# The feed-forward layer of a fused Perceiver kernel: both products as three fp32r passes, accumulated tile by tile in four banks

## The chip, the cores and the metric

The kernel runs on one core of one Trainium2 chip. The metric is the device time of one launch in microseconds (us). The engines are PE (TensorE, matrix products), ACT (ScalarE), DVE (VectorE), POOL (GpSimd) and SP (SyncE, which issues the DMAs). Each runs its own instruction list in order; they wait for each other through semaphores.

## What is computed

Six layers act on 1024 tokens of width 512 (16 batches of 64), one after the other: a cosine cross-attention, a self-attention, a mixture of experts, a cross-attention, a decayed attention and a feed-forward layer. Only the last one matters here. Its part of the reference, in short:

```python
def pwlin_gelu_basic(x, mantissa_bits_in, mantissa_bits_out):
    xq = float2fix(x, mantissa_bits_in)          # rounded to multiples of 2^-8
    y = jnp.interp(xq, _PWL_X, _PWL_Y)           # exact GELU at 33 knots on [-4, 4]
    y = jnp.where(xq > 4.0, xq, jnp.where(xq < -4.0, 0.0, y))
    return float2fix(y, mantissa_bits_out)

h = layernorm(x) @ w1 + b1        # w1 is 512 x 2048
h = pwlin_gelu_basic(h, 8, 8)
y = float2fix(h @ w2 + b2, 8)     # w2 is 2048 x 512
out = x + y
```

All of it is fp32. The tokens lie in SBUF as 8 tiles `x[:, t, :]` of 128 tokens by 512.

## The kernel before

`feed_forward_layer` splits the tokens into two groups of four tiles (`NGR` = 2, `TG` = 4) and the inner width into 16 tiles of 128 (`FT`). One step n, of `N` = 32, is one inner tile of one group: 128 inner rows by 512 tokens. A step is this pipeline:

- PE, `hidden(n)`: four fp32 products `w16` by `xT[g]` into PSUM bank n mod 3.
- ACT, `stage_a(n)`: `h` (L2004) out of PSUM, then `r` (L2009), both 128x512.
- DVE, `round_(n)`: `c` (L2047) and `up` (L2051), clamped forms of `r`.
- ACT, `stage_b(n)`: `km` (L2019, the knot), then GELU at both neighbouring knots, `g0` (L2022) and `g1` (L2024).
- POOL, `slope(n)`: `dg` = g1 - g0 (L1943).
- DVE, `interpolate(n)`: three operations on `y` (L2060, L2063, L2065; the second one waits for `dg`) and then `hs` (L2067), the finished inner tile.
- PE, `output(t, f0, f1)`: token tile t by the inner tiles f0 to f1-1, fp32, into bank 3 + t mod 3.

The inner tiles of both groups are kept in SBUF (`hs`, 2 x 16 tiles). The order on PE is written out by hand: the transposes of the first group's normalized tokens, the 16 `hidden` steps of group 0 (with the transposes of group 1 at four places among them), then 16 times a `hidden` step of group 1 and four `output` products of group 0, and last the 64 `output` products of group 1. DVE and ACT interleave two steps: DVE runs `round_(n + 1)` ahead of `interpolate(n)`, ACT `stage_a(n + 1)` ahead of `stage_b(n)`. `Norm` computes the layer norm: DVE statistics (L134 to L137), a power on POOL (L142), `xn` on DVE (L148), four transposes on PE (L155) into bank 7, and a copy `xT` on ACT (L1998). DVE normalizes the second group's tiles after steps 1, 3, 5 and 7. `finish(t)` takes an output tile out of PSUM with three DVE operations (L2075, L2077, L2078), and SP stores it with two DMAs.

`split_product` (L103, used by other layers before and by this one after) does an fp32 product as three passes of the faster type fp32r: with each operand as a first part (rounded to fp32r) and a rest, it adds first x first, first x rest and rest x first. ACT makes the first part by a copy, DVE the rest by a subtraction.

At the start of the layer's block SP issues the loads of `b1`, `w26` (4 MB) and `b2`, in this order; DVE waits for both biases before it does anything else in the layer. `w16` is loaded during the layer before.

## Time and profile before

| | us |
|---|---|
| median of 3 runs (2247.7 to 2256.31) | 2249.49 |
| the profiled execution's own time | 2252.86 |
| its span, from first to last instruction | 2251.0 |
| PE busy over the span | 2014.5 |
| DVE busy | 1085.9 |
| ACT busy | 914.2 |
| POOL busy | 100.5 |

The feed-forward layer is the last eighth: its loads are issued at 1983.7 us of the span, and the program ends at 2251.0. A row of the timeline gives start, duration, engine, line and operation, with what it writes and reads; in square brackets stands how long the engine had been idle before it and who ended that. Operations of one engine overlap by their tails, so the distance of two starts can be under the first one's duration. A PE row merges several matmuls. An fp32 product is recorded as two matmuls, an fp32r product as one.

### The profile page before, as it was taken

How to read it: one execution, taken by the hardware profiler on the slowest of the kernel's cores; microseconds unless marked ns; L12 is line 12 of the kernel's file. 1: busy time of each engine (PE TensorE's matmuls, PEld its weight loads, DVE VectorE, ACT ScalarE, POOL GpSimd, SP SyncE). 2: the span in 40 equal slices, each digit the busy share in tenths (PEclk: the TensorE clock that was granted, in tenths of full speed). 3: DMA queues.
4: the chain of work that ended last, by engine and by line, in shares of the span. 5: the costliest groups of instructions: out<-in, count | busy, mean ns of one | idle time of the engine just before them, and what ended most of it. 6: DMA issues, size and time to landing. Idle time of an engine off the chain costs nothing. (4 is left out here: it accounts for less than half of the span.)

```text
span 2251.0 us, 29109 instructions
## 1 busy us (share of the span) xinstructions
PE 2014.5 (89%) x9936; PEld 1418.6 (63%) x9936; DVE 1085.9 (48%) x2233; ACT 914.2 (41%) x1684; POOL 100.5 (4%) x113
## 2 busy tenths in 40 slices
PE   7978963999999959999999999999968898858998
PEld 5647763555555547777778787878746676623443
DVE  5665651001010127363544445363538899929852
ACT  5743320111111125353544444454526667726650
POOL 0000002000000001000000000000000000002220
PEclk9989875999999989999999999999988888779999
DMA  7410006777777622110101100000212000020000
GB/s 266 135 46 1 0 17 245 289 313 312 293 297 313 261 71 76 38 47 14 47 14 47 43 31 33 28 33 28 75 63 103 1 1 1 1 80 1 5 10 24
DMA packets 33156, 208.19 MB, mean 92 GB/s; under 512 B 4546, under 2 KB 4674, under 8 KB 25540
## 3 DMA queue, kind: packets, MB, share of 16 engines
q1 hardware_dynamic: 30532, 199.02, 23.5%
q0 software_dynamic: 2560, 8.39, 1.1%
q8 instruction: 31, 0.51, 0.1%
q14 instruction: 33, 0.27, 0.0%
HBM read 186.95 MB, written 20.45 MB: 92 GB/s over the span
## 5 line engine op out<-in xcount | busy, mean ns | idle before, releaser
L109 PE MATMUL PS<-cT,qs 128*128 128x512 f32 x1152 | 293.9, 401 | 9.0 <-ACT pb L1259 7.0
L109 PE MATMUL PS<-pT,cN 128*128 128x512 f32 x1152 | 271.8, 394 | 1.7 <-DVE pT L1354 1.7
L109 PEld LDWEIGHTS PS<-cT,qs 128*128 128x128 f32 x1152 | 208.6, 188 | 59.3 <-issue 15.0
L917 PE MATMUL PS<-W,xgT 128*128 128x384 f32 x736 | 243.7, 490 | 1.4 <-ACT xgT L940 1.4
L109 PEld LDWEIGHTS PS<-pT,cN 128*128 128x128 f32 x1152 | 215.1, 189 | 45.8 <-DVE pT L1354 1.9
L917 PEld LDWEIGHTS PS<-W,xgT 128*128 128x128 f32 x736 | 141.1, 192 | 104.4 <-issue 12.1
L109 PE MATMUL PS<-ws,xT 128*128 128x512 f32 x672 | 180.4, 427 | 6.4 <-DVE ws L563 4.9
L109 PEld LDWEIGHTS PS<-ws,xT 128*128 128x128 f32 x672 | 137.6, 207 | 45.8 <-issue 11.5
L1349 DVE TENSOR_REDUCE nmax<-PS 128x1 f32<-128x512 f32 x128 | 87.7, 685 | 156.0 <-PE PS L109 155.6
L968 DVE TENSOR_TENSOR hid<-gated,PS 128x384 f32<-128x384 f32 x46 | 23.4, 551 | 278.4 <-PE PS L893 235.6
L1254 ACT ACTIVATE qp<-PS 128x512 f32<-128x512 f32 x96 | 57.4, 598 | 191.4 <-PE PS L109 191.4
L901 PE MATMUL PS<-W,hT 128*128 128x512 f32 x276 | 124.5, 601 | 10.3 <-ACT hT L934 10.3
L1962 PE MATMUL PS<-xT,W 128*128 128x512 f32 x256 | 118.4, 613 | 1.3 <-ACT xT L1998 0.8
L1354 DVE TENSOR_TENSOR pT<-PS,pT 128x512 fp32r<-128x512 f32 x128 | 86.9, 684 | 54.6 <-ACT pT L1276 54.6
L947 ACT ACTIVATE gated<-PS 128x384 f32<-128x384 f32 x46 | 20.0, 488 | 228.2 <-PE PS L917 228.2
L1972 PE MATMUL PS<-W,hs 128*128 128x512 f32 x256 | 112.5, 592 | 0.0
L1566 PEld LDWEIGHTS PS<-cn,W 128*128 128x128 f32 x512 | 77.8, 225 | 39.0 <-DVE W L1878 31.6
L155 PE MATMUL PS<-cn,xn 128*128 128x128 f32 x160 | 28.8, 310 | 81.9 <-DVE xn L148 72.9
L1276 ACT ACTIVATE pT<-PS 128x512 fp32r<-128x512 f32 x128 | 75.6, 597 | 64.3 <-PE PS L1154 64.1
L1259 ACT ACTIVATE pb<-PS,nmax 128x512 f32<-128x512 f32 x128 | 87.5, 684 | 34.5 <-DVE nmax L1349 34.4
L1566 PE MATMUL PS<-cn,W 128*128 128x16 f32 x512 | 76.6, 284 | 24.2 <-DVE W L1878 24.0
L901 PEld LDWEIGHTS PS<-W,hT 128*128 128x128 f32 x276 | 50.6, 190 | 70.7 <-issue 56.9
(231 smaller groups left out, 3096.5 us busy)
## 6 DMA issues: line engine op xcount, KB each, us to landing
W<-in_fc SPq DMA_DIRECT2D x23, 3072.0 KB, 12.4
W<-in_proj SPq DMA_DIRECT2D x23, 1536.0 KB, 6.5
cT<-in_ctxT SPq DMA_DIRECT2D x16, 768.0 KB, 5.2
ct_in<-in_ctxT SPq DMA_DIRECT2D x16, 768.0 KB, 4.2
cn_in<-in_ctxN SPq DMA_DIRECT2D x16, 768.0 KB, 5.1
W<-in_w SPq DMA_DIRECT2D x2, 4096.0 KB, 12.9
routed_x<-zero SPq DMA_DIRECT2D x23, 256.0 KB, 5.4
xg<-routed_x SPq DMA_DIRECT2D x23, 256.0 KB, 5.6
```

The source lines that it names most:

```text
L109: mm = nc.tensor.matmul(out, lhs(m, s), rhs(n, s), start=(opens and (s, m, n) == terms[0]), stop=((s, m, n) == terms[-1]))
L155: last = self.nc.tensor.transpose(self.bank[:, k * P:(k + 1) * P], self.xn[:, k * P:(k + 1) * P], self.ident)
L901: mm = nc.tensor.matmul(ps[7], hT[:, f, :], pj[u][:, f, :], start=(f == 0), stop=(f == FK - 1))
L917: mm = nc.tensor.matmul(ps[c][:, 0:HFE], xgT[:, k, :], fc[u][:, k, c * HFE:(c + 1) * HFE], start=(k == 0), stop=(k == DK - 1))
L1254: nc.scalar.activation(out, src, ACT.Copy, scale=scale).then_inc(w_sb, count)
L1259: nc.scalar.activation(pb[:, g % 2, :], ps[g % 2], ACT.Exp, bias=nmax[:, g % 4:g % 4 + 1], accum_out=rsum[:, g % 4:g % 4 + 1]).then_inc(e_ ...
L1276: nc.scalar.activation(turned(pT[0], g), ps[2 + g % 2].rearrange("p (j n) -> p j n", j=JK), ACT.Copy).then_inc(pt_hi, 1)
L1349: nc.vector.tensor_reduce(nmax[:, g % 4:g % 4 + 1], ps[g % 2], AX.X, ALU.max, negate=True).then_inc(m_dve, 1)
L1354: return nc.vector.tensor_tensor(out, whole, first.bitcast(F32), ALU.subtract)
L1566: mm = nc.tensor.matmul(ps[6 + c % 2][:, col:col + B], rb[:, t % RB, k * P:(k + 1) * P], sel, start=True, stop=True)
L1962: mm = nc.tensor.matmul(ps[n % HB], w16[:, k, f * P:(f + 1) * P], xT[g][:, k, :], start=(k == 0), stop=(k == DK - 1))
L1972: mm = nc.tensor.matmul(ps[HB + t % ZB], hs[:, t // TG, f, (t % TG) * P:(t % TG + 1) * P], w26[:, f, :], start=(f == 0), stop=(f == FT - 1))
```

## The change

The whole change is inside `feed_forward_layer`. Both products go through three fp32r passes. The inner tile is no longer kept: each step's finished `hs` is split into `hp` (first part by ACT, L2037, rest by DVE, L2112), and PE multiplies it four steps later (`LAG`) by the matching rows of `w26` into four banks at once, one for each token tile of the group, which accumulate over the 16 steps of a group. The weights are split for each step as well, into rings of three: `ws` for the first product (ACT L2004, DVE L2107, two steps ahead) and `vs` for the second (ACT L2044, DVE L2117). The normalized tokens are split as they leave PSUM (`rest_x`). Since a weight is split again in each group, every step has three more copies on ACT and three more subtractions on DVE. The group's four banks are read by `sum_out` (L2126) in one go after step 18, and finished one each after steps 19 to 22; those of the second group at the end. `b2` is loaded ahead of `w26`, and DVE waits for the biases after the norms of the first four tiles.

How the steady step's rows move on two engines. First DVE, one step of the second group, as it stood before (`c`, `up`: clamps of the next step; `y`, `hs`: this step's interpolation):

```order
L2047 TENSOR_SCALAR c<-r 128x512
L2051 TENSOR_SCALAR up<-r 128x512
L2060 SCALAR_TENSOR_TENSOR y<-km,c 128x512
L2063 SCALAR_TENSOR_TENSOR y<-y,dg 128x512
L2065 SCALAR_TENSOR_TENSOR y<-g,y 128x512
L2067 SCALAR_TENSOR_TENSOR hs<-y,up 128x512
```

and as it stands now, where `ws`, `hp` and `vs` are the rests of the first weight, of the inner tile and of the second weight:

```order
L2117 TENSOR_TENSOR vs<-W,vs 128x512
L2075 TENSOR_SCALAR c<-r 128x512
L2079 TENSOR_SCALAR up<-r 128x512
L2107 TENSOR_TENSOR ws<-W,ws 128x512
L2112 TENSOR_TENSOR hp<-hs,hp 128x512
L2089 SCALAR_TENSOR_TENSOR y<-km,c 128x512
L2092 SCALAR_TENSOR_TENSOR y<-y,dg 128x512
L2094 SCALAR_TENSOR_TENSOR y<-g,y 128x512
L2096 SCALAR_TENSOR_TENSOR hs<-y,up 128x512
```

Between one step's `hs` and the next one's first `y` DVE had two operations; now it has five. On ACT, one step before:

```order
L2004 ACTIVATE h<-PS,b1q 128x512
L2009 ACTIVATE r<-h,cn 128x512
L2019 ACTIVATE km<-c,cn 128x512
L2022 ACTIVATE g<-km,cn 128x512
L2024 ACTIVATE g<-km,cn 128x512
```

and now, where `ws`, `hp` and `vs` are the first parts:

```order
L2004 ACTIVATE ws<-W 128x512
L2010 ACTIVATE h<-PS,b1q 128x512
L2015 ACTIVATE r<-h,cn 128x512
L2037 ACTIVATE hp<-hs 128x512
L2025 ACTIVATE km<-c,cn 128x512
L2028 ACTIVATE g<-km,cn 128x512
L2030 ACTIVATE g<-km,cn 128x512
L2044 ACTIVATE vs<-W 128x512
```

The copy `hp<-hs`, which waits for `hs` of the step before, stands ahead of `km` and the two GELUs. Before, nothing on ACT waited for `hs` of the step before.

The diff, without the declarations of semaphores and the removed bodies of `output` and `finish`, which the listing of the kernel before shows:

```diff
--- before.py
+++ after.py
...
-        hs = sbuf("hs6", [P, NGR, FT, 512])
-        xT = [sbuf(f"xT6{g}", [P, DK, TG * P]) for g in range(NGR)]
+        WR, LAG = 3, 4
+        hs = sbuf("hs6", [P, 2, 512])
+        hp = [sbuf(f"hp6{part}", [P, WR, 512], F32R) for part in range(2)]
+        vs = [sbuf(f"vs6{part}", [P, WR, D], F32R) for part in range(2)]
+        xT = [[sbuf(f"xT6{g}{part}", [P, DK, TG * P], F32R) for part in range(2)] for g in range(NGR)]
+        ws = [sbuf(f"ws6{part}", [P, WR, DK, P], F32R) for part in range(2)]
+        z = sbuf("z6", [P, TG, D])
...
-        z = x[:, NT, :]
...
-        TURN_LAG, OUT_LAG = 6, 4
+        TURN_LAG, OUT_LAG = 4, 3
...
                 sp.dma_start(b1[:, :], a["b16"]).then_inc(s_b, 16)
+                sp.dma_start(b2[:, :], a["b26"]).then_inc(s_b, 16)
                 sp.dma_start(w26, a["w26"]).then_inc(s_w26, 16)
-                sp.dma_start(b2[:, :], a["b26"]).then_inc(s_b, 16)
...
                     g, f = divmod(n, FT)
                     if f == 0:
                         pe.wait_ge(ln.xT_ready, BASE + TG * (g + 1))
+                    pe.wait_ge(w_lo, BASE + n + 1)
                     if n >= HB:
                         pe.wait_ge(h_sb, BASE + n - HB + 1)
-                    for k in range(DK):
-                        mm = nc.tensor.matmul(ps[n % HB], w16[:, k, f * P:(f + 1) * P], xT[g][:, k, :],
-                                              start=(k == 0), stop=(k == DK - 1))
-                    mm.then_inc(h_mm, 1)
-                def output(t, f0, f1):
...
+                    split_product(nc, ps[n % HB], lambda part, k: ws[part][:, n % WR, k, :],
+                                  lambda part, k: xT[g][part][:, k, :], DK).then_inc(h_mm, 1)
+                def output(n):
+                    g, f = divmod(n, FT)
+                    pe.wait_ge(hp_lo, BASE + n + 1)
+                    pe.wait_ge(v_lo, BASE + n + 1)
+                    for t in range(TG):
+                        if g and f == 0:
+                            pe.wait_ge(z_used, BASE + t + 1)
+                        for m, r in ((0, 0), (0, 1), (1, 0)):
+                            mm = nc.tensor.matmul(ps[HB + t], hp[m][:, n % WR, t * P:(t + 1) * P], vs[r][:, n % WR, :],
+                                                  start=(f == 0 and m == r), stop=(f == FT - 1 and m == 1))
+                    mm.then_inc(o_mm, 1)
...
-                for n in range(FT):
+                for n in range(N):
                     hidden(n)
                     if n - TURN_LAG in NORM_AT:
                         ln.tensor(pe, TG + NORM_AT.index(n - TURN_LAG))
...
+                    if n >= LAG:
+                        output(n - LAG)
+                for n in range(N - LAG, N):
+                    output(n)
...
                     act.wait_ge(ln.turned, BASE + t + 1)
-                    part = xT[t // TG][:, :, t % TG * P:(t % TG + 1) * P]
-                    nc.scalar.activation(part, ps[7].rearrange("p (k t) -> p k t", k=DK),
-                                         ACT.Copy).then_inc(ln.xT_ready, 1)
+                    part = xT[t // TG][0][:, :, t % TG * P:(t % TG + 1) * P]
+                    nc.scalar.activation(part, ps[7].rearrange("p (k t) -> p k t", k=DK), ACT.Copy).then_inc(x_hi, 1)
+                def first_w(n):
+                    if n >= WR:
+                        act.wait_ge(h_mm, BASE + n - WR + 1)
+                    nc.scalar.activation(ws[0][:, n % WR, :, :], w16[:, :, n % FT * P:(n % FT + 1) * P],
+                                         ACT.Copy).then_inc(w_hi, 1)
...
+                def first_h(n):
+                    act.wait_ge(hs_sb, BASE + n + 1)
+                    if n >= WR:
+                        act.wait_ge(o_mm, BASE + n - WR + 1)
+                    nc.scalar.activation(hp[0][:, n % WR, :], hs[:, n % 2, :], ACT.Copy).then_inc(hp_hi, 1)
+                def first_v(n):
+                    if n == 0:
+                        act.wait_ge(s_w26, BASE + 16)
+                    if n >= WR:
+                        act.wait_ge(o_mm, BASE + n - WR + 1)
+                    nc.scalar.activation(vs[0][:, n % WR, :], w26[:, n % FT, :], ACT.Copy).then_inc(v_hi, 1)
+                act.wait_ge(e.s_w6, BASE + 16)
+                first_w(0)
+                first_w(1)
                 for t in range(TG):
                     norm_out(t)
                 act.wait_ge(b_q, BASE + 2)
                 stage_a(0)
                 for n in range(N):
+                    if n + 2 < N:
+                        first_w(n + 2)
                     if n + 1 < N:
                         stage_a(n + 1)
+                    if n:
+                        first_h(n - 1)
                     stage_b(n)
+                    first_v(n)
                     if n - OUT_LAG in NORM_AT:
                         norm_out(TG + NORM_AT.index(n - OUT_LAG))
+                first_h(N - 1)
...
                     ve.wait_ge(km_sb, BASE + n + 1)
                     if n >= 2:
                         ve.wait_ge(hs_sb, BASE + n - 1)
+                        ve.wait_ge(hp_lo, BASE + n - 1)
...
-                    nc.vector.scalar_tensor_tensor(hs[:, g, f, :], y[:, u, :], ROUND, up[:, u, :], ALU.add,
+                    nc.vector.scalar_tensor_tensor(hs[:, u, :], y[:, u, :], ROUND, up[:, u, :], ALU.add,
                                                    ALU.add).then_inc(hs_sb, 1)
+                def rest_x(t):
+                    ve.wait_ge(x_hi, BASE + t + 1)
+                    hi, lo = (part[:, :, t % TG * P:(t % TG + 1) * P] for part in xT[t // TG])
+                    nc.vector.tensor_tensor(lo, ps[7].rearrange("p (k t) -> p k t", k=DK), hi.bitcast(F32),
+                                            ALU.subtract).then_inc(ln.xT_ready, 1)
+                def rest_w(n):
+                    ve.wait_ge(w_hi, BASE + n + 1)
+                    nc.vector.tensor_tensor(ws[1][:, n % WR, :, :], w16[:, :, n % FT * P:(n % FT + 1) * P],
+                                            ws[0][:, n % WR, :, :].bitcast(F32), ALU.subtract).then_inc(w_lo, 1)
+                def rest_h(n):
+                    ve.wait_ge(hp_hi, BASE + n + 1)
+                    nc.vector.tensor_tensor(hp[1][:, n % WR, :], hs[:, n % 2, :], hp[0][:, n % WR, :].bitcast(F32),
+                                            ALU.subtract).then_inc(hp_lo, 1)
+                def rest_v(n):
+                    ve.wait_ge(v_hi, BASE + n + 1)
+                    nc.vector.tensor_tensor(vs[1][:, n % WR, :], w26[:, n % FT, :], vs[0][:, n % WR, :].bitcast(F32),
+                                            ALU.subtract).then_inc(v_lo, 1)
+                def sum_out(t):
+                    g = t // TG
+                    ve.wait_ge(o_mm, BASE + FT * (g + 1))
+                    if g:
+                        ve.wait_ge(x_done, BASE + t - TG + 1)
+                    nc.vector.tensor_tensor(z[:, t % TG, :], ps[HB + t % TG], b2[:, :], ALU.add).then_inc(z_used, 1)
                 def finish(t):
+                    zt = z[:, t % TG, :]
+                    ve.wait_ge(z_used, BASE + t + 1)
+                    ch.link(nc.vector.tensor_scalar(zt, zt, ROUND, ROUND, ALU.add, ALU.subtract))
+                    nc.vector.scalar_tensor_tensor(x[:, t, :], zt, 1.0 / QUANT, x[:, t, :], ALU.mult,
+                                                   ALU.add).then_inc(x_done, 1)
+                for t in range(TG):
+                    ln.vector_stats(ch, t)
                     if t:
...
+                        rest_x(t - 1)
+                    ln.vector_norm(ve, t)
                 ve.wait_ge(s_b, BASE + 32)
                 nc.vector.tensor_scalar(b1q[:, :], b1[:, :], QUANT, None, ALU.mult).then_inc(b_q, 1)
                 nc.vector.tensor_scalar(b2[:, :], b2[:, :], QUANT, None, ALU.mult).then_inc(b_q, 1)
-                for t in range(TG):
-                    ln.vector_stats(ch, t)
-                    ln.vector_norm(ve, t)
+                rest_w(0)
+                rest_w(1)
+                rest_x(TG - 1)
                 round_(0)
                 for n in range(N):
                     if n + 1 < N:
                         round_(n + 1)
+                    if n + 2 < N:
+                        rest_w(n + 2)
+                    if n:
+                        rest_h(n - 1)
                     interpolate(n)
+                    rest_v(n)
                     if n in NORM_AT:
                         ln.vector_stats(ch, TG + NORM_AT.index(n))
                         ln.vector_norm(ve, TG + NORM_AT.index(n))
...
+                    if n - OUT_LAG in NORM_AT:
+                        rest_x(TG + NORM_AT.index(n - OUT_LAG))
+                    if n == FT + 2:
+                        for t in range(TG):
+                            sum_out(t)
+                    elif FT + 3 <= n < FT + 3 + TG:
+                        finish(n - FT - 3)
+                rest_h(N - 1)
+                for t in range(TG, NT):
+                    sum_out(t)
                     finish(t)
```

## Rows read from the trace of the kernel before

**Rows 1.** Windows: stretch, us, busy PE, PEld, DVE, ACT, POOL, then PEclk, DMA.

```profile
2026.64:2197.73 171.09, 162.15 (x383) 71.41 (x382) 134.14 (x210) 100.84 (x152) 42.05 (x35) 0.99 0.02 5
2197.73:2251.00 53.27, 47.54 (x111) 20.75 (x109) 8.96 (x16) 0.00 (x0) 0.00 (x0) 0.98 0.08 25
```

**Rows 2.** Chain that ended last: start, us, what.

```profile
2101.07 3.43 PE PS L1962 x8
...
2189.91 55.38 PE PS L1972 x129
```

**Rows 3.** Timeline from the layer's loads to the first finished step.

```profile
1983.71 0.33 SPq L1926 DMA_DIRECT2D b<-in_b  x1
...
1997.01 0.18 DVE L2082 TENSOR_SCALAR b1q<-b 128x16 f32<-128x16 f32 x1 [14.51 <-DMA b<-in_b]
...
1997.43 0.69 DVE L134 BATCH_NORM_STATS2 st<-x 128x6 f32<-128x512 f32 x1
...
1999.30 0.55 DVE L148 TENSOR_SCALAR xn<-x,mv,rs 128x512 f32<-128x512 f32 x1 [0.66 <-POOL rs L142]
...
2001.05 0.60 ACT L1998 ACTIVATE xT<-PS 128x512 f32<-128x512 f32 x1 [23.03 <-PE PS L155]
...
2008.77 21.54 PE L1962 MATMUL PS<-xT,W 128*128 128x512 f32 x44 [0.78 <-ACT xT L1998]
...
2025.95 0.69 DVE L2067 SCALAR_TENSOR_TENSOR hs<-y,up 128x512 f32<-128x512 f32 x1
```

**Rows 4.** Timeline of PE in the cross-attention: a dense fp32r stream.

```profile
1617.59 8.46 PE L109 MATMUL PS<-pT,cN 128*128 128x512 f32 x36
1625.89 2.21 PE L109 MATMUL PS<-cT,qs 128*128 128x512 f32 x9
```

**Rows 5.** Timeline in the cross-attention: splits into first part and rest.

```profile
1071.51 0.63 ACT L1267 ACTIVATE cT<-ct_in 128x512 fp32r<-128x512 f32 x1
1071.80 0.68 DVE L1354 TENSOR_TENSOR cT<-ct_in,cT 128x512 fp32r<-128x512 f32 x1
1072.04 0.68 ACT L1259 ACTIVATE pb<-PS,nmax 128x512 f32<-128x512 f32 x1
```

**Rows 6.** Timeline of one feed-forward step: DVE, ACT, POOL.

```profile
2107.33 0.41 DVE L2047 TENSOR_SCALAR c<-r 128x512 f32<-128x512 f32 x1
...
2107.78 0.72 ACT L2019 ACTIVATE km<-c,cn 128x512 f32<-128x512 f32 x1 [0.98 <-DVE c L2047]
2108.00 0.68 DVE L2060 SCALAR_TENSOR_TENSOR y<-km,c 128x512 f32<-128x512 f32 x1
...
2109.17 0.71 ACT L2024 ACTIVATE g<-km,cn 128x512 f32<-128x512 f32 x1
...
2109.95 1.31 POOL L1943 TENSOR_TENSOR dg<-g 128x512 f32<-128x512 f32 x1 [3.09 <-ACT g L2024]
2110.17 1.64 DVE L2067 SCALAR_TENSOR_TENSOR hs<-y,up 128x512 f32<-128x512 f32 x1
```

**Rows 7.** Timeline a step later: POOL starts while DVE is in an operation.

```profile
2114.57 0.69 DVE L2067 SCALAR_TENSOR_TENSOR hs<-y,up 128x512 f32<-128x512 f32 x1
...
2114.91 1.48 POOL L1943 TENSOR_TENSOR dg<-g 128x512 f32<-128x512 f32 x1 [3.65 <-ACT g L2024]
...
2115.18 1.49 DVE L2047 TENSOR_SCALAR c<-r 128x512 f32<-128x512 f32 x1
```

**Rows 8.** Timeline of PE at an idle time.

```profile
2070.85 0.63 PE L155 MATMUL PS<-cn,xn 128*128 128x128 f32 x4 [3.02 <-ACT xT L1998]
2071.34 12.56 PE L1962 MATMUL PS<-xT,W 128*128 128x512 f32 x24
```

**Rows 9.** Windows of PE just behind it: us, busy, PEclk.

```profile
2072.00:2074.00 2.00, 2.00 (x4) 0.50 0.00 0
```

**Rows 10.** Timeline of DVE: the last output tile.

```profile
2245.37 0.69 DVE L2075 TENSOR_TENSOR x<-PS,b 128x512 f32<-128x512 f32 x1 [11.85 <-PE PS L1972]
...
2246.56 0.69 DVE L2078 SCALAR_TENSOR_TENSOR x<-x 128x512 f32<-128x512 f32 x1
```

More of the change, by code:

```diff
@@ L1912, in feed_forward_layer @@
             sem(n) for n in ("h_mm6", "h_sb6", "r_sb6", "c_sb6", "km_sb6", "g_sb6", "up_sb6", "dg_sb6", "hs_sb6"))
-        z_mm, z_used, x_done, s_out = sem("z_mm6"), sem("z_used6"), sem("x_done6"), sem("s_out6")
+        o_mm, z_used, x_done, s_out = sem("o_mm6"), sem("z_used6"), sem("x_done6"), sem("s_out6")
+        x_hi, w_hi, w_lo = sem("x_hi6"), sem("w_hi6"), sem("w_lo6")
+        hp_hi, hp_lo, v_hi, v_lo = sem("hp_hi6"), sem("hp_lo6"), sem("v_hi6"), sem("v_lo6")
         s_w26 = sem("s_w26")
         N = NGR * FT
-        HB, ZB = 3, 3
+        HB = 3
         NORM_AT = [1 + 2 * t for t in range(TG)]
-        TURN_LAG, OUT_LAG = 6, 4
+        TURN_LAG, OUT_LAG = 4, 3
         e.open_sems()
@@ L1958, in hidden @@
                         pe.wait_ge(ln.xT_ready, BASE + TG * (g + 1))
+                    pe.wait_ge(w_lo, BASE + n + 1)
                     if n >= HB:
                         pe.wait_ge(h_sb, BASE + n - HB + 1)
-                    for k in range(DK):
-                        mm = nc.tensor.matmul(ps[n % HB], w16[:, k, f * P:(f + 1) * P], xT[g][:, k, :],
-                                              start=(k == 0), stop=(k == DK - 1))
-                    mm.then_inc(h_mm, 1)
-                def output(t, f0, f1):
-                    if f0 == 0 and t >= ZB:
-                        pe.wait_ge(z_used, BASE + t - ZB + 1)
-                    for f in range(f0, f1):
-                        pe.wait_ge(hs_sb, BASE + FT * (t // TG) + f + 1)
-                        mm = nc.tensor.matmul(ps[HB + t % ZB], hs[:, t // TG, f, (t % TG) * P:(t % TG + 1) * P],
-                                              w26[:, f, :], start=(f == 0), stop=(f == FT - 1))
-                    if f1 == FT:
-                        mm.then_inc(z_mm, 1)
+                    split_product(nc, ps[n % HB], lambda part, k: ws[part][:, n % WR, k, :],
[11 more added lines that the diff above has]
+                    mm.then_inc(o_mm, 1)
                 for t in range(TG):
                     ln.tensor(pe, t)
-                pe.wait_ge(e.s_w6, BASE + 16)
-                for n in range(FT):
+                for n in range(N):
                     hidden(n)
@@ L1983, in _ @@
                         ln.tensor(pe, TG + NORM_AT.index(n - TURN_LAG))
-                per = FT // TG
-                pe.wait_ge(s_w26, BASE + 16)
-                for f in range(FT):
-                    hidden(FT + f)
-                    output(f // per, f % per * per, (f % per + 1) * per)
-                for t in range(TG, NT):
-                    output(t, 0, FT)
+                    if n >= LAG:
+                        output(n - LAG)
+                for n in range(N - LAG, N):
+                    output(n)
             @block.scalar
@@ L2094, in _ @@
                         ln.vector_norm(ve, TG + NORM_AT.index(n))
-                    per = FT // TG
-                    if n >= FT + 1 and (n - FT) % per == 1 and (n - FT) // per >= 1:
-                        finish((n - FT) // per - 1)
-                for t in range(TG - 1, NT):
+                    if n - OUT_LAG in NORM_AT:
[8 more added lines that the diff above has]
+                    sum_out(t)
                     finish(t)
```

7 lines of the change are left out of this document (removed).

## Prediction

> **What bounds the kernel now.** The edit lies in the last eighth of the span, so I read that layer alone, in three views. The windows cut it in three. From the end of the first finished inner tile (`hs` of step 0, 2026.64) to that of the last (2197.73) both PE and DVE are loaded: PE 162.15 and DVE 134.14 of 171.09 us. After that DVE is nearly empty (8.96) and PE alone works for 53.27 us [rows 1]. The chain that ended last is there PE and nothing else: 129 records of the second product in 55.38 us, and further up alternating blocks of 8 records at 3.43 us. A record is thus 0.429 us, an fp32 product two of them, 0.86 us; a step of the second half, four products in and four out, is 6.86 us of PE [rows 2]. The timeline shows a third stretch ahead of both: DVE stands 14.51 us, to 1997.01, for a bias that is queued behind the 4 MB of `w26`; the first product starts at 2008.77 [rows 3].
>
> **The layer's start.** Without that wait the norms can start right after the loads are issued at 1983.71; I take 1984.0. The first `xn` comes 1.87 later (1997.43 to 1999.30 before), the copy out of PSUM 1.75 after its `xn`, and takes 0.60 [rows 3]. New is the rest on DVE, 0.68 for this shape [rows 5], and the next `xn` stands behind it: a tile now takes 1.75 + 0.60 + 0.03 + 0.61 = 3.0. So four tiles end at 1984.0 + 1.87 + 3 x 3.0 + 1.75 + 0.60 + 0.72 = 1997.9, and PE starts 10.8 earlier. From there to the first `hs` before took 2025.95 + 0.69 - 2008.77 = 17.9 [rows 3]. PE starts at half clock either way; 12 fp32r products (below) take 5.1 there against the 6.2 of the four fp32 ones. With the next weight's rest ahead of the first `y` I get 16.5, so `hs` of step 0 ends at **2014.4**. `w26` is first needed at about 2010; before, a transfer queued behind it had landed by 1997.
>
> **The steady step.** PE: in the cross-attention 36 fp32r matmuls of 128x512 start at 1617.59 and the next group at 1625.89: 8.30 us, 0.231 each [rows 4]. A step has 24, so 5.53 us instead of 6.86. The fp32r passes do save, but only 1.33 per step.
>
> DVE gets three subtractions of 0.68, each 0.61 to the next start (0.61 is the distance from `hs` to `c`) [rows 5, 7]. Its other work: `c` and `up` 0.67 together (2107.33 to 2108.00), the three `y` 2.17 (2108.00 to 2110.17), `hs` 0.61 [rows 6, 7]. Sum: 0.67 + 2.17 + 0.61 = 3.45 old, + 1.83 new = 5.28. That alone would be under PE's 5.53. But a step also has POOL's `dg`, 1.27 when it is not held up (the 1.48 less the 0.21 until the `hs` of 2114.57 has run 0.55), and DVE and POOL do not run side by side here: `hs` that starts 0.22 after `dg` takes 1.64 instead of 0.69 [rows 6], and `dg` that starts inside an `hs` takes 1.48, with the `c` behind it 1.49 instead of 0.41 [rows 7]. Each time the later one ends as if it had begun when the other let go (about 0.55 into a DVE operation). The Trainium skill (SBUF — State Buffer, section "SBUF: two separate sides") has the rule: GpSimd's operation and a VectorE operation with two SBUF inputs take one shared port pair exclusively. By it every new subtraction of the weights and of `hs` is of the kind that cannot overlap `dg`; the trace agrees for the old ones.
>
> Where does `dg` fall now? ACT's new order puts the copy of `hs` of the step before ahead of `km`. Counted from the end of that `hs`: copy at 0.03, 0.53 long to the next start [rows 5], `km`, 1.39 to `g1` (2107.78 to 2109.17), 0.71 for it, 0.07 to POOL [rows 6]: `dg` asks at 2.73. DVE by then: the second weight's rest from -0.08, `c` 0.53, `up`, the first weight's rest 1.20, the rest of `hs` 1.81, `y` 2.42. `dg` gets in when that `y` lets go, 2.97, ends at 4.24, and the second `y` starts about 0.1 later, 4.34; `hs` ends 1.45 + 0.69 later: **6.48 us a step**. Bounds: 6.23 if `dg` could run beside `y` (2.73 + 1.27 + 0.10 + 2.14, ACT's chain alone), 6.9 if handoffs cost what nothing here shows. I take 6.48, since rows 6 and 7 both show the exclusion. So the step's limit moves from PE to a loop DVE - ACT - POOL - DVE, and ACT, nearly idle before, is in it.
>
> A second loop stays just below: first weight's rest ends 1.89, 12 products take 2.94, `h` and `r` some 1.45, and the next copy of `hs` stands behind `r` on ACT: at 6.26, where the first loop has it at 6.48 + 0.03. It has 0.25 to spare.
>
> **What is added on top.** Four norms stand between `hs` and the next `c`: 1.87 + 0.46 [rows 3] and nothing covers them; they also delay the weight's rest by as much, so that `r` is 1 us late a step on: another 0.7. Less small overlaps 2.9 each, 11.6, and 0.6 for the last `rest_x`: 12.2. The four `sum_out` in a row (4 x 0.61) cost 2.3 and the four `finish` 1.0 each: 6.2. The last two steps lack weights to split, -0.5. Steps: 31 x 6.48 = 200.9; together 218.8, against 171.1 before.
>
> **Clock.** PE idles long wherever DVE hands over a weight late: in a step behind a norm the weight's rest ends at 5.3 after `hs` instead of 1.9, while PE has run out of work at about 1.2, so 4 us. That is so ahead of products 2, 3 and 4 (no output products to fill in yet), behind three norms and behind `sum_out`. One idle of 3.02 before was followed by a granted clock of 0.50, the 1.2 GHz level, and 24 records took 12.56 where 24 x 0.429 = 10.3: about 2.1 lost [rows 8, 9]. I take three such drops of some seven chances, 6.3, since they fall on the second loop, which has no room: last `hs` at 2014.4 + 218.8 + 6.3 = **2239.5**. The Trainium skill (TensorE: Matmul & The Clock Gate, section "What's actually happening") says that idleness brings the lower level and activity the higher; by it all seven would drop, which is the second rival below.
>
> **The end.** Where 53.3 us of PE stood alone, only one step is left: copy and rest of `hs` 1.4, 12 products 2.9, then four output tiles on DVE at (2246.56 - 2245.37) + 0.61 = 1.8 each, 7.3, and from the end of DVE's last operation (2247.25) to 2251.0 as before 3.75 [rows 10]: 15.4.
>
> **Sum**, against the profiled execution's own span of 2251.0: start -12.2, steps 218.8 + 6.3 - 171.1 = +54.0, end 15.4 - 53.3 = -37.9: **+3.9**, span 2254.9. The median of the runs shown is 1.5 below that span, so I predict 2253. A difference of 0.5%, 11 us, is about what a measurement of this kernel can tell from none: 2238 to 2261 is "same".
>
> **Rivals.**
> - *Faster* (0.20): `dg` overlaps the subtractions after all, the step is 6.23, and DVE's idle 0.7 a step soaks up part of norms and sums (9 x 0.7): 31 x 6.23 + 18.4 - 6.3 = 205.2 instead of 218.8, and later weights come earlier, so few drops: 2235 span, 2234. For it: no subtraction from fp32 to fp32r ran beside a `dg` before. Against: rows 6 and 7.
> - *Slower by the clock* (0.17): each of the idle times drops the clock, and the 0.95 us of idle in ordinary steps brings some more, 12 in all: +9 x 2.1, 2272. It decides from seven drops on. For it: rows 8 and 9. Against: PE is busy 85% of a step, more than the stretches behind which no drop shows.
> - *Slower by the handoffs* (0.15): a step has six more waits between ACT, DVE and PE; 0.3 us a step of them on either loop is +9.3, 2263. For it: both loops are full. Against: the waits in rows 6 cost 0.03 to 0.10 each and are in the sum.
> - *The forecast* (0.48): own range 2243 to 2264.
>
> **How the numbers follow.** The forecast's case gives 0.02 faster, 0.40 same, 0.06 slower; the faster rival 0.20 faster; the clock 0.14 slower and 0.03 same; the handoffs 0.15 slower. Together 0.22, 0.43, 0.35. The range leaves out about one in ten on either side: 2233 takes in the faster rival, 2275 the clock's.
>
> **What would show it.** First `hs` ending near 2014; `hs` 6.5 apart in steps 10 to 17 and 24 to 29, with the second `y` waiting for POOL about 1.2 and `dg` taking about 1.5 (0.25 of it waiting); PE busy 85% there; norms 9 us a step; 15 us after the last `hs`. It is wrong if `hs` stands 6.25 or 6.8 apart, if PEclk is under 0.9 over the layer, or if the norms still start at 1997.

## The result, and the profile after

The changed kernel takes 2258.18 us (median of 20 runs, 2255.22 to 2262.49), the kernel before 2253.59 in the same series (median of 20). One launch of the kernel before took 7014.76 us and does not enter the ratio. The ratio is 1.0026, with a 95% interval of 1.0019 to 1.0033: slower by a quarter of a per cent, 5.8 us by the means and 4.6 by the medians, which is inside the 0.5% that the prediction called "same". Forecast were 2253 us, and a chance of 0.43 for "same". Of the 5.2 us between that forecast and the measured 2258.18, 4.1 are the base: the forecast started from a median of 2249.49 for the kernel before, which is 2253.59 over 20 runs.

The profiled run took 2256.09 us, its span is 2254.2. The page's line of busy times for it:

```profile
PE 1985.5 (88%) x10192; PEld 1469.4 (65%) x10192; DVE 1137.1 (50%) x2337; ACT 967.3 (43%) x1780; POOL 104.1 (5%) x113
```

PE has 29 us less work than before, DVE 51 and ACT 53 us more. The saving on PE was real and bought nothing.

The layer's length is the measure here: from SP's first load to the end of the span it was 2251.0 - 1983.71 = 267.3 us. Now, from the timeline around the layer's first load:

```profile
1981.40 0.33 SPq L1931 DMA_DIRECT2D b<-in_b  x1
1981.45 0.69 DVE L134 BATCH_NORM_STATS2 st<-x 128x6 f32<-128x512 f32 x1 [1.56 <-PEq L2222]
1983.32 0.55 DVE L148 TENSOR_SCALAR xn<-x,mv,rs 128x512 f32<-128x512 f32 x1 [0.66 <-POOL rs L142]
```

The wait of 14.51 us for the bias [rows 3] is gone: the statistics start 0.05 behind the load's issue. The length is 2254.2 - 1981.40 = 272.8, 5.5 more than before. (That the layer begins 2.3 earlier than in the profile of before is no effect of the edit, nothing ahead of it changed; over all runs here this point lies between 1977.5 and 1985.3.)

One step of the second group, the timeline of DVE, ACT, POOL and PE:

```profile
2106.57 0.69 DVE L2096 SCALAR_TENSOR_TENSOR hs<-y,up 128x512 f32<-128x512 f32 x1
...
2107.30 0.63 ACT L2037 ACTIVATE hp<-hs 128x512 fp32r<-128x512 f32 x1
...
2109.20 3.06 PE L109 MATMUL PS<-xT,ws 128*128 128x512 f32 x12 [0.73 <-DVE ws L2107]
2109.66 0.69 DVE L2089 SCALAR_TENSOR_TENSOR y<-km,c 128x512 f32<-128x512 f32 x1
...
2109.99 1.50 POOL L1948 TENSOR_TENSOR dg<-g 128x512 f32<-128x512 f32 x1 [4.98 <-ACT g L2030]
...
2111.60 0.69 DVE L2092 SCALAR_TENSOR_TENSOR y<-y,dg 128x512 f32<-128x512 f32 x1 [1.26 <-POOL dg L1948]
...
2113.05 0.69 DVE L2096 SCALAR_TENSOR_TENSOR hs<-y,up 128x512 f32<-128x512 f32 x1
```

Two `hs` stand 2113.05 - 2106.57 = 6.48 apart, and so they do (6.47 to 6.49) in steps 12 to 18 and 24 to 29, a step being counted from the `hs` before to its own. In this one `dg` takes 1.50 instead of the 1.27 that it needs alone, and the second `y` stands 1.26 for it. PE, once the bound, waits 0.73 for the weight's rest. The waits over the whole layer (who waited for whom: total, times, longest) tell the same:

```profile
ACT h L2010 <- PE PS L109: 66.0, 32, 6.7
...
PE PS L109 <- DVE ws L2107: 37.3, 26, 4.2
DVE y L2092 <- POOL dg L1948: 34.0, 24, 2.7
```

The first is idle time of ACT, which binds nothing in the steady steps. The second and third are PE and DVE, the two loaded engines, both waiting now.

### The profile page after: what moved, and what is told of

It is laid out like the page before. It is cut to its first block and busy times, and to the rows that moved or that the text cites. A ratio compares the mean times of both kernels' runs of the same rounds, so it can differ in the third digit from the quotient of the medians.

```text
span 2254.2 us, 29909 instructions
## 1 busy us (share of the span) xinstructions
PE 1985.5 (88%) x10192; PEld 1469.4 (65%) x10192; DVE 1137.1 (50%) x2337; ACT 967.3 (43%) x1780; POOL 104.1 (5%) x113
## 5 line engine op out<-in xcount | busy, mean ns | idle before, releaser
L109 PE MATMUL PS<-xT,ws 128*128 128x512 f32 x384 | 108.7, 438 | 39.5 <-DVE ws L2107 37.3
L109 PEld LDWEIGHTS PS<-xT,ws 128*128 128x128 f32 x384 | 78.3, 211 | 69.0 <-DVE ws L2107 49.3
L1979 PE MATMUL PS<-vs,hp 128*128 128x512 f32 x384 | 97.3, 405 | 7.1 <-DVE hp L2112 4.3
```

The source lines that it names most:

```text
L109: mm = nc.tensor.matmul(out, lhs(m, s), rhs(n, s), start=(opens and (s, m, n) == terms[0]), stop=((s, m, n) == terms[-1]))
L1979: mm = nc.tensor.matmul(ps[HB + t], hp[m][:, n % WR, t * P:(t + 1) * P], vs[r][:, n % WR, :], start=(f == 0 and m == r), stop=(f == FT - 1 ...
```

## The experiments

A ratio is always to the kernel before, run on the same chip. "First to last `hs`" is the distance between the first and the last finished inner tile: 171.1 us before [rows 1], 225.6 after.

**1. The new start alone, on the kernel before.**

```diff
-                sp.dma_start(w26, a["w26"]).then_inc(s_w26, 16)
                 sp.dma_start(b2[:, :], a["b26"]).then_inc(s_b, 16)
+                sp.dma_start(w26, a["w26"]).then_inc(s_w26, 16)
...
-                ve.wait_ge(s_b, BASE + 32)
-                nc.vector.tensor_scalar(b1q[:, :], b1[:, :], QUANT, None, ALU.mult).then_inc(b_q, 1)
-                nc.vector.tensor_scalar(b2[:, :], b2[:, :], QUANT, None, ALU.mult).then_inc(b_q, 1)
                 for t in range(TG):
...
                     ln.vector_norm(ve, t)
+                ve.wait_ge(s_b, BASE + 32)
+                nc.vector.tensor_scalar(b1q[:, :], b1[:, :], QUANT, None, ALU.mult).then_inc(b_q, 1)
+                nc.vector.tensor_scalar(b2[:, :], b2[:, :], QUANT, None, ALU.mult).then_inc(b_q, 1)
```

> The kernel before with the start of the new one alone: b2 loaded ahead of w26, and the biases awaited after the first four norms. Theory: the norms start some 13.5 us earlier, the whole layer behind them shifts, 13 us less than before (ratio 0.994). Rival: the earlier start is given back at a later wait (the second weight's load, the DVE-bound first half): no difference.

Measured: 2236.76, ratio 0.9933 (0.9919 to 0.9946). First to last `hs` is 171.1 as before; the gain is all ahead of it. The first `hs` starts 28.6 us after the loads' issue instead of 42.2, 13.7 earlier. The start is worth 15 us by the ratio (12 to 18 by its interval).

**2. New start and new order of PE's work, but both products in fp32 and nothing split** (a ring of 16 `hs`).

```diff
-                for n in range(FT):
+                for n in range(N):
                     hidden(n)
...
+                    if n == LAG:
+                        pe.wait_ge(s_w26, BASE + 16)
+                    if n >= LAG:
+                        output(n - LAG)
+                for n in range(N - LAG, N):
+                    output(n)
```

> The new start and the new order (output product of each step four steps later, four banks, sums after step 18), but both products stay fp32 and nothing is split. Theory: PE is then busy without a break at 6.86 us a step and only one step and four sums are left at the end: 20 us less than before (ratio 0.991), while the fp32r version is 0.26% slower, so the three passes and not the order take the time away. Rival: the order itself is what costs (sums in a row, four banks, waits): no better than before.

Measured: 2232.43, 0.9907 (0.9891 to 0.9922). In the steady steps PE works without a break, eight records (four products) of either kind every 3.43 us, 6.87 a step. From its timeline:

```profile
2150.15 3.60 PE L1963 MATMUL PS<-xT,W 128*128 128x512 f32 x8
2153.58 3.60 PE L1974 MATMUL PS<-W,hs 128*128 128x512 f32 x8
```

So the order costs nothing; it gives another 0.0026. The two intervals just meet, but the layers of the profiled runs say the same: 248.2 us here, 253.7 in number 1. From 0.9907 to 1.0026 the difference is the three passes with their splits and buffers (and the second group's transposes, placed two steps earlier on PE and one on ACT, which was not tried alone): they cost 0.0119, 27 us, though each step of PE needs 1.3 us less.

**3. A second subtraction on POOL behind each `dg`**, of `b2` from itself into a place that nothing reads. It leaves the result as it is.

```diff
+                    if n == 0:
+                        pool.wait_ge(b_q, BASE + 2)
+                    if n:
+                        pool.wait_ge(s_idle, BASE + n)
+                    nc.gpsimd.tensor_tensor(idle, b2[:, :], b2[:, :], ALU.subtract).then_inc(s_idle, 1)
```

> The changed kernel with a second, unused POOL subtraction of the same size behind each dg; nothing waits for it. Theory (DVE and POOL exclude each other): DVE's y or hs of that moment is held up by it, the steady step goes from 6.48 to 7.4 to 7.8 us, 30 to 40 us more. Rival (the step is ACT's and POOL's latency alone): the step stays 6.48, since the added operation lies in POOL's idle time.

Measured in a single run: 2280.37; a step takes 7.22 to 7.25, and the layer is 27.0 us longer than in the changed kernel where I expected 30 to 40. From the timeline of DVE and POOL:

```profile
2119.91 1.52 POOL L1949 TENSOR_TENSOR dg<-g 128x512 f32<-128x512 f32 x1 [4.72 <-ACT g L2036]
...
2121.39 1.04 POOL L1955 TENSOR_TENSOR x<-b 128x512 f32<-128x512 f32 x1
2121.53 1.44 DVE L2098 SCALAR_TENSOR_TENSOR y<-y,dg 128x512 f32<-128x512 f32 x1 [1.27 <-POOL dg L1949]
```

Nobody waits for the added operation, and yet DVE's `y`, starting 0.14 behind it, takes 1.44 instead of 0.69. That is the step's whole increase, 0.75. It came out under the 7.4 to 7.8 that I expected; this subtraction took 1.04, not 1.27, which accounts for 0.23 of it. The exclusion that the prediction took from rows 6 and 7 is there.

**4. `dg` computed by DVE instead of POOL**, whose `slope(n)` is gone.

```diff
-                    ve.wait_ge(dg_sb, BASE + n + 1)
+                    ve.wait_ge(g_sb, BASE + 2 * n + 2)
+                    ch.link(nc.vector.tensor_tensor(dg[:, u, :], g1[:, u, :], g0[:, u, :], ALU.subtract))
+                    ve.sem_inc(dg_sb, 1)
```

> The changed kernel with dg computed by DVE instead of POOL. Theory: dg costs DVE 0.72 instead of 1.27 plus handoffs plus 0.25 of waiting; DVE's own work becomes 6.0 us a step and the second loop (weight rest, 12 products, h, r, copy of hs) binds at 6.2: 8 to 10 us less than the changed kernel, so even with before (ratio 0.998 to 1.000). Rival (DVE's sum of work is already the limit): the step gets longer by 0.6, 20 us more than the changed kernel (ratio 1.011).

Measured: 2241.32, 0.9948 (0.9934 to 0.9961), 17 us under the changed kernel and about twice the 8 to 10 that I expected. One step of DVE, from its timeline:

```profile
2115.88 0.68 DVE L2110 TENSOR_TENSOR vs<-W,vs 128x512 fp32r<-128x512 f32 x1
2116.48 0.42 DVE L2066 TENSOR_SCALAR c<-r 128x512 f32<-128x512 f32 x1
2116.82 0.42 DVE L2070 TENSOR_SCALAR up<-r 128x512 f32<-128x512 f32 x1
2117.15 0.68 DVE L2100 TENSOR_TENSOR ws<-W,ws 128x512 fp32r<-128x512 f32 x1
2117.76 0.68 DVE L2105 TENSOR_TENSOR hp<-hs,hp 128x512 fp32r<-128x512 f32 x1
2118.36 0.68 DVE L2080 SCALAR_TENSOR_TENSOR y<-km,c 128x512 f32<-128x512 f32 x1
2119.07 0.69 DVE L2083 TENSOR_TENSOR dg<-g 128x512 f32<-128x512 f32 x1
2119.91 0.69 DVE L2085 SCALAR_TENSOR_TENSOR y<-y,dg 128x512 f32<-128x512 f32 x1
2120.64 0.69 DVE L2087 SCALAR_TENSOR_TENSOR y<-g,y 128x512 f32<-128x512 f32 x1
2121.37 0.69 DVE L2089 SCALAR_TENSOR_TENSOR hs<-y,up 128x512 f32<-128x512 f32 x1
2121.98 0.68 DVE L2110 TENSOR_TENSOR vs<-W,vs 128x512 fp32r<-128x512 f32 x1
```

No row has a wait in brackets: DVE alone fills 2121.98 - 2115.88 = 6.10. On DVE `dg` costs 0.84 to the next start, on POOL it kept DVE away for 1.26 more than its own work. What I had expected to stop the step at 6.26, the "second loop", does not.

**5. ACT's copy of `hs` behind the GELUs, its rest behind the interpolation**; `dg` stays on POOL.

```diff
+                    stage_b(n)
                     if n:
                         first_h(n - 1)
-                    stage_b(n)
...
+                    interpolate(n)
                     if n:
                         rest_h(n - 1)
-                    interpolate(n)
```

> The changed kernel with ACT's copy of hs moved behind km and the two GELUs, and its rest on DVE behind the interpolation. Theory: hs is out of the loop, but then r, c, the weight's rest, 12 products, h and r close a loop of 5.83 us, dg comes late after r, and DVE does rests and dg one after the other: about 6.6 a step, 0 to 5 us more than the changed kernel (ratio to before 1.003 to 1.005). Rival (the copy of hs ahead of the GELUs alone sets the 6.48): the step falls to about 5.8, 20 us less (ratio 0.994).

Measured: 2262.91, 1.0043 (1.0029 to 1.0057); the step 6.48 to 6.49, not the 6.6 that I expected. From the timeline:

```profile
2123.67 0.71 ACT L2030 ACTIVATE g<-km,cn 128x512 f32<-128x512 f32 x1
2124.20 0.68 DVE L2089 SCALAR_TENSOR_TENSOR y<-km,c 128x512 f32<-128x512 f32 x1
2124.29 0.62 ACT L2037 ACTIVATE hp<-hs 128x512 fp32r<-128x512 f32 x1
...
2124.46 1.59 POOL L1948 TENSOR_TENSOR dg<-g 128x512 f32<-128x512 f32 x1 [4.89 <-ACT g L2030]
```

With the copy out of ACT's chain, `dg` asks a little earlier and is held up longer (1.59 against 1.50), behind the same first `y`; what stands behind it on DVE waits as before. So the copy's place on ACT, which I had named as what puts ACT into the loop, does not set 6.48. The edit slackened ACT's chain by less than the copy, though: `dg` starts 2.65 after the end of the `hs` before where it was 2.73, since ACT now has `r` directly ahead of `km` (2121.67 and 2122.30). What numbers 4 and 5 leave is a sum: DVE's own work and `dg` stand in series. The loop is 3.7 us longer than in the changed kernel. Two of its steps take 9.86 and 9.85: in each PE idles 3.09, its next 12 products take 5.49, and DVE's `c` waits 2.01 and 3.08 for ACT's `r`.

**6. Both edits**, `dg` on DVE and the copy late.

```diff
+                    if n >= 2:
+                        rest_h(n - 2)
+                    if n:
+                        rest_v(n - 1)
+                    ve.wait_ge(g_sb, BASE + 2 * n + 2)
+                    ch.link(nc.vector.tensor_tensor(dg[:, u, :], g1[:, u, :], g0[:, u, :], ALU.subtract))
```

> dg on DVE, ACT's copy of hs behind the GELUs, and the rests of hs (two steps back) and of the second weight (one step back) between the first y and dg. Theory: nothing is left but DVE's own work, 6.0 us a step: 12 to 15 us less than the changed kernel (ratio to before 0.996 to 0.997). Rival: some other loop (PE at 5.53 plus waits) holds it at 6.4 or more: no better than the changed kernel.

Measured: 2242.5, 0.9955 (0.9941 to 0.9969), steps of 6.09 to 6.10. Giving the chain more slack gains nothing: DVE's work is the limit. The gain on the changed kernel is 16 us where I expected 12 to 15.

**7. Three passes for the first product only**, the second in fp32 from a ring of 8 `hs`: two splits less per step.

```diff
-                        for m, r in ((0, 0), (0, 1), (1, 0)):
-                            mm = nc.tensor.matmul(ps[HB + t], hp[m][:, n % WR, t * P:(t + 1) * P], vs[r][:, n % WR, :],
-                                                  start=(f == 0 and m == r), stop=(f == FT - 1 and m == 1))
+                        mm = nc.tensor.matmul(ps[HB + t], hs[:, n % HR, t * P:(t + 1) * P], w26[:, f, :],
+                                              start=(f == 0), stop=(f == FT - 1))
```

> The changed kernel with only the first product in three fp32r passes; the second is fp32 out of a ring of eight finished inner tiles, so the splits of hs and of the second weight are gone. Theory: DVE has 4.06 plus dg, PE 2.77 + 3.43 = 6.2 a step and binds, norms are mostly covered: 25 to 30 us less than before (ratio 0.987 to 0.989), the best of these. Rival: the loop through the weight's rest and r holds it at 6.5 as well: ratio 1.00.

Measured: 2237.51, 0.9928 (0.9915 to 0.9940). The steady step is PE's again, 6.16 to 6.17, but I expected 0.987 to 0.989: steps with a norm and the ones behind them still take 7.4 to 7.5. The timeline of one of these shows why:

```profile
2052.91 0.55 DVE L148 TENSOR_SCALAR xn<-x,mv,rs 128x512 f32<-128x512 f32 x1 [0.66 <-POOL rs L142]
...
2053.77 1.48 POOL L1946 TENSOR_TENSOR dg<-g 128x512 f32<-128x512 f32 x1 [0.89 <-ACT g L2028]
2054.04 1.76 DVE L2089 TENSOR_TENSOR ws<-W,ws 128x512 fp32r<-128x512 f32 x1
...
2055.85 2.37 PE L109 MATMUL PS<-xT,ws 128*128 128x512 f32 x9 [1.75 <-DVE ws L2089]
```

The norm makes the weight's rest late, the rest falls into a `dg` and takes 1.76 instead of 0.68, and PE stands 1.75 for it.

**8. The changed kernel with PE kept busy in its long idle times** by up to 4 fp32 products ahead of seven `hidden` steps, and 3 ahead of the last `output`. What they write is never read.

```diff
+                FILL = {2: 3, 3: 4, 4: 4, 6: 4, 8: 4, 10: 4, 21: 4}
...
+                    for _ in range(FILL.get(n, 0)):
+                        nc.tensor.matmul(ps[n % HB], ident, cn[:, 0:512], start=True, stop=True)
+                    pe.wait_ge(w_lo, BASE + n + 1)
...
+                    if n == N - 1:
+                        for _ in range(3):
+                            nc.tensor.matmul(ps[7], ident, cn[:, 0:512], start=True, stop=True)
```

> The changed kernel with 3 or 4 unused fp32 products on PE in each of its long idle times (ahead of first products 2, 3, 4, 6, 8, 10, 21 and of the last output step). Theory: the granted clock stays at the upper level there, steps 3 to 11 and the last step get their 1.4 to 2.5 us each back as far as they lie in the loop: 7 to 10 us less than the changed kernel (ratio to before 0.998 to 0.999). Rival: the drops are hidden behind DVE and only the last counts: 2 us less.

Measured: 2253.73, 0.9999 (0.9990 to 1.0007), 6 us under the changed kernel; 7 to 10 were expected. Windows of PE (stretch, its length, busy time and count, granted clock, DMA share, GB/s), first in the changed kernel, then with the fill:

```profile
2004.00:2024.00 20.00, 12.56 (x31) 0.69 0.01 1
...
2056.00:2064.00 8.00, 7.18 (x19) 0.57 0.00 0
...
2234.00:2244.00 10.00, 5.79 (x14) 0.66 0.00 0
```

```profile
2004.00:2024.00 20.00, 16.38 (x50) 1.00 0.00 1
...
2056.00:2064.00 8.00, 7.37 (x29) 1.00 0.00 0
...
2234.00:2244.00 10.00, 5.78 (x19) 0.96 0.02 4
```

The clock stays up at seven of the eight places (at the `sum_out` not by the fill, which stands behind an idle time of 2.81 there). Behind three of the norms a step is shorter by 1.5, 2.5 and 1.5 us: DVE's `c`, which waited 1.56, 2.47 and 1.46 there for ACT's `r`, does not wait at all. The end, from the start of the last `hs`, is shorter by 2.4 (16.4 for 18.8). Two places took some of that back. The step with the first norm is followed by one that is 1.1 longer: with the drop ahead of it gone, `dg` comes earlier and holds up the clamp `c` (1.49), the weight's rest stays late, PE idles 3.43 behind its fill, and the next 12 products still take 4.49. And at the `sum_out` the fill, 3.59 us of PE, stood in the way of the next products: 1.8 longer.

**9. Number 7 with the first weight split three steps ahead**, in a ring of four.

```diff
-        WR, LAG = 3, 4
+        WR, LAG = 4, 4
...
-                    if n + 2 < N:
-                        first_w(n + 2)
+                    if n + 3 < N:
+                        first_w(n + 3)
...
-                    if n + 2 < N:
-                        rest_w(n + 2)
+                    if n + 3 < N:
+                        rest_w(n + 3)
```

> First product fp32r, second fp32, as in the run with the first alone, and the first weight split three steps ahead instead of two, in a ring of four. Theory: the norm pairs cost 14.8 us there because the weight's rest comes late and r after it; with one more step of lead only the norm's own work on DVE is left: 4 to 6 us less than that run (ratio to before 0.990 to 0.991). Rival (DVE's exclusion with POOL alone makes the norm steps long): no change, 0.993.

Measured: 2222.67, 0.9871 (0.9854 to 0.9888), 13 us under number 7 by the ratios, where I expected 4 to 6. A norm now costs its own step (7.33), and the one behind it is back at 5.0 to 5.5. First to last `hs` falls from 203.4 to 189.1.

**10. Number 9 with `dg` on DVE**, by the edit of number 4.

> The same with dg on DVE as well. Theory: DVE has 4.9 us a step and 7.2 in a norm step, the lead covers those, and PE works without a break at 6.17: 8 to 10 us less than the run with the first product alone (ratio to before 0.988 to 0.989), less than the all-fp32 order (0.991). Rival: the 0.7 us that DVE takes over lengthen each norm step: 0.992 or more.

Measured: 2218.71, 0.9853 (0.9838 to 0.9868): 33 us faster than before, and the lowest of all, though its interval overlaps that of number 9. Under number 7 it is 17 us where I expected 8 to 10. PE has one long idle time left in the layer, 3.21 us ahead of the fourth inner tile's products, and none of more than 0.8 at a norm. From its timeline, that idle time and one norm's transposes:

```profile
2011.63 3.01 PE L109 MATMUL PS<-xT,ws 128*128 128x512 f32 x12 [3.21 <-DVE ws L2083]
...
2035.26 0.63 PE L155 MATMUL PS<-cn,xn 128*128 128x128 f32 x4 [0.62 <-DVE xT L2078]
2035.73 3.60 PE L1968 MATMUL PS<-W,hs 128*128 128x512 f32 x8
```

**11. The changed kernel with the old start.** The edit of number 1, backwards.

> The changed kernel with the old start: b2 loaded behind w26, and the biases awaited ahead of the norms. Theory: the start is worth here what it was worth in the kernel before (15 us), as nothing later can take it up: ratio to before 1.008 to 1.010. Rival (the start's gain is hidden behind the load of w26 or the split of the first weights): no more than the changed kernel, 1.003.

Measured: 2273.78, 1.0094 (1.0079 to 1.0109); first to last `hs` 225.35. The start is worth 0.0068 here and 0.0067 in number 1: it adds to the rest, on either kernel.

## Why the prediction was right, and where its sum was off

**What it comes out of.** Three parts with signs of their own: the start -0.0067 (number 1), the order -0.0026 (number 2 against number 1), the three passes with their splits +0.0119. The prediction had +3.9 us in all; the layer of the profiled run is 5.5 longer.

**The layer's start.** -12.2 forecast for the first finished `hs`. Counted from the loads' issue it ends at 2010.50 - 1981.40 = 29.1, before at 2026.64 - 1983.71 = 42.9: -13.8. PE's first product came 11.4 earlier where 10.8 was forecast, and a norm takes 2.98 a tile where I had 3.0. Right, a little too cautious.

**The steady step.** 6.48 forecast, 6.48 measured, with the second `y` waiting 1.26 ("about 1.2") and `dg` at 1.50 ("about 1.5"). PE is busy 5.75 of 6.48, 89% where I had 85%. `dg` asked 2.73 after `hs`, as forecast. The two halves of the reasoning fared differently. That `dg` and DVE's operations exclude each other held in numbers 3, 5 and 7. Of the loop DVE - ACT - POOL - DVE, ACT was no part that matters, and the forecast's own sum says so: `dg` asks at 2.73 and gets in at 2.97, when `y` lets go, so ACT has 0.24 to spare. Measured `dg` is held up 0.23 in the changed kernel and 0.32 in number 5, where it asks 0.08 earlier, with the step at 6.48 in both, and with `dg` on DVE the step was DVE's bare work, 6.10. DVE's work without `dg` is 6.10 - 0.84 = 5.26 (number 4), and around `dg` two starts of `y` stand 1.94 apart (2109.66 and 2111.60) instead of 0.71 (2118.36 and 2119.07 in number 4), 1.23 more: 6.49, the step. "A second loop stays just below: at 6.26" was wrong: number 4, which has that loop too, runs at 6.10, so it is at most that.

**What is added on top.** 12.2 for the norms, 6.2 for sums and finishes, and 6.3 for the clock, less 0.5 for the last two steps. Measured against 6.48 a step: 19.0 for steps 1 to 11, in which the norms lie, with their clock; 6.1 for the sums and finishes (8.60 and 7.68 for two steps, then 7.42, 7.43, 7.41), with theirs; -0.4 at the end. The price of a norm can be read without the clock in number 8: the last three pairs of a norm's step and the one behind it are 3.4, 3.0 and 3.0 over two steady steps, where 2.9 was forecast. First to last `hs` is 225.6 where 218.8 + 6.3 = 225.1 was forecast.

**Clock.** "Three such drops of some seven chances" was wrong as a count. The granted clock over the layer, from 1995.0 on, was 0.91, just above the 0.9 that was named as a sign of being wrong. All the long idle times were followed by the lower level; the timeline of PE shows the first two and the longest one, and between them 12 products at the upper level:

```profile
2005.09 4.46 PE L109 MATMUL PS<-xT,ws 128*128 128x512 f32 x12 [2.93 <-DVE ws L2107]
2012.47 5.49 PE L109 MATMUL PS<-xT,ws 128*128 128x512 f32 x12 [2.93 <-DVE ws L2107]
...
2028.93 3.02 PE L109 MATMUL PS<-xT,ws 128*128 128x512 f32 x12 [0.21 <-DVE ws L2107]
...
2056.82 5.49 PE L109 MATMUL PS<-xT,ws 128*128 128x512 f32 x12 [4.16 <-DVE ws L2107]
```

Twelve products take 3.02 at the 2.4 GHz level and 4.46 to 5.49 here; there are eight such places. The Trainium skill (TensorE: Matmul & The Clock Gate, section "What's actually happening") has idleness bring the lower level and activity the higher; by that rule every one of my seven chances would drop, and the trace of this kernel agrees (other kernels here show exceptions, below). But the size came out right: the loop pays 0.5 us more than forecast in all. Number 8 shows the price where the drop was taken away cleanly: 1.5, 2.5 and 1.5 behind three norms, 5.5 together. The one behind the `sum_out` cost 0.14: that step took 7.68, and 7.54 in number 11, where no drop came. What the first three cost was not measured and stays open; since the loop came out at 225.6, all seven in it cost about 225.6 - 218.8 = 6.8, an estimate that holds if the other terms are right. So the forecast of 6.3 came out by luck, by two errors that cancelled: more places and less at each.

**The end** is the term that was mis-sized. 15.4 forecast, 2254.2 - 2236.11 = 18.1 measured. The timeline of PE at its last two steps:

```profile
2231.29 3.01 PE L1979 MATMUL PS<-vs,hp 128*128 128x512 f32 x12 [1.05 <-DVE hp L2112]
2237.55 5.49 PE L1979 MATMUL PS<-vs,hp 128*128 128x512 f32 x12 [3.25 <-DVE hp L2112]
```

I priced the last 12 products at 2.9 and did not see that, with no `hidden` step left, PE idles ahead of them for 3.25 us and then runs at the lower level: 5.49, +2.6. Number 8 took 2.4 of it back. With the start 1.6 better, the steps 0.5 and the end 2.7 worse, +3.9 becomes the measured +5.5.

**The rivals.** *Faster*, at 0.20, needed `dg` to run beside the subtractions. It fell: a weight's rest inside a `dg` took 1.76 instead of 0.68 (number 7), and work added on POOL that nobody waits for cost 0.75 a step (number 3). The Trainium skill (SBUF — State Buffer, section "SBUF: two separate sides") gives GpSimd and a VectorE operation with two SBUF inputs one port pair exclusively; the trace agrees with it now for the new subtractions too. *Slower by the clock* counted twelve drops at 2.1 each and said that it decides from seven on. Eight came, seven of them in the loop, so its deciding condition was met; it fell by their price, about 1 us each on the path there. *Slower by the handoffs* fell: the step is 6.48, not 6.8.

**Where the saving went.** From the end of the first `hs` to the end of the program, PE was busy 162.15 + 47.54 = 209.7 of 224.4 us before [rows 1]. The same two windows of the changed kernel (PE, PEld, DVE, ACT, POOL, then the clock, DMA share, GB/s):

```profile
2010.50:2236.11 225.61, 185.73 (x736) 142.72 (x736) 181.85 (x309) 153.35 (x246) 46.18 (x35) 0.94 0.02 5
2236.11:2254.20 18.09, 5.49 (x12) 3.81 (x12) 8.26 (x14) 0.63 (x1) 0.00 (x0) 0.62 0.18 58
```

PE is busy 191.2 of 243.7: 18.5 less work, part of it at the lower clock, and 52.5 of idle time where there were 14.7. Before, PE was seldom kept waiting, and the 53 us at the end in which it worked alone were no waste. Now 32 steps are paced by DVE, whose six operations became nine: 3.45 us of work became 5.26, and with `dg` in series 6.49, over PE's 5.53. Number 10 keeps the passes for the first product alone, which needs one split on DVE per step and not three, and there PE sets the pace again, at 6.16 instead of 6.87.

## What to carry to other kernels

A cheaper product is worth only what its operands cost where they are made: count, per step, the splits on the engine that is next to the bound, and split only the operand that pays for itself (here the one with a single subtraction a step). When POOL and DVE work in alternation, add POOL's time to DVE's work instead of laying them side by side, and try the operation on DVE: here 1.26 became 0.84. Prepare an operand one step further ahead than the steady step needs, since an interruption of one engine (a norm) otherwise reaches PE and lets it idle, and in the changed kernel (idle times of 3.78 to 4.16 at the norms) a clock drop came on top, while in number 7 (1.70 to 1.75) none did; and look for such an idle time at the very end, where the pipeline drains.

## What the runs showed of the hardware

An operation on POOL whose result nobody reads lengthened DVE's `y` from 0.69 to 1.44 us, so that an unused operation of 1.04 cost 0.75 a step. Operations with one tensor input are held up as well: the clamp `c`, 0.42 alone, took 1.49 when it started while `dg` ran. The timeline of the changed kernel at a norm:

```profile
2036.34 1.33 POOL L1948 TENSOR_TENSOR dg<-g 128x512 f32<-128x512 f32 x1 [0.37 <-ACT g L2030]
2036.46 1.49 DVE L2075 TENSOR_SCALAR c<-r 128x512 f32<-128x512 f32 x1
```

The length of an idle time does not settle by itself whether the clock falls. In the changed kernel it fell behind all eight of 2.84 to 4.16 us and behind none of up to 1.93. But two norms of number 4 were ahead of these rows of PE:

```profile
2043.17 3.06 PE L109 MATMUL PS<-xT,ws 128*128 128x512 f32 x12 [2.22 <-DVE ws L2100]
...
2058.28 4.40 PE L109 MATMUL PS<-xT,ws 128*128 128x512 f32 x12 [2.23 <-DVE ws L2100]
```

2.22 us without a drop, 2.23 with one. The kernel before shows it too: of its idle times at the norms 2.43 and 3.01 brought none and 3.02 did, the one that the forecast took its price from. Ahead of the products behind `sum_out` it was 2.84 with a drop in the changed kernel, 2.81 without in number 8 and 2.89 without in number 11; the 3.21 of number 10 was followed by 12 products in 3.01. In number 6 the clock fell at the end behind only 1.81 (granted clock 0.79 and 0.64 in two stretches of 3 us from 2216 on, 1.00 after that). Over all kernels here, idle times of 1.8 to 3.2 us in the layer went either way, and every one of 3.23 us or more brought a drop. I can't say from these runs what decides in between.
